# Local attention writes its result twice, and the linear attention takes its turned tokens from the second copy by GpSimd and VectorE

## The reference, cut to what matters

```
x = x + local_attention(group_norm(x))
t = tokens(x)                                   # 16 x 3136 x 128
t = t + linear_attention(ln(t), W, b)           # q,k = elu(.)+1; running sums of k v^T and k over t
t = t + recurrence(ln(t), W, V, gamma, beta)    # y = sigmoid(BN(W ln(t)) + V y), step by step
```

## Time and profile before

| | us |
|---|---|
| median of 3 runs | 1787.8 (1784.03 to 1788.23) |
| the profiled execution | 1784.76 |
| its span, first to last instruction | 1782.8 |
| TensorE / VectorE / ScalarE / GpSimd busy | 1749.7 / 1509.8 / 1269.8 / 1073.7 |
| mean granted clock of TensorE | 0.996 of full speed |

### The profile page before, as it was taken

How to read it: one execution, slowest core, us unless ns; L and a number is a source line. 1 busy time by engine, 2 the same in 40 slices (tenths; PEclk the granted TensorE clock), 3 DMA queues, 4 the chain that set the end, 5 groups by cost and what they waited for, 6 DMA issues and landing times.

```text
span 1782.8 us, 58142 instructions
## 1 busy us (share of the span) xinstructions
PE 1749.7 (98%) x19648; PEld 1587.7 (89%) x19648; DVE 1509.8 (85%) x4546; ACT 1269.8 (71%) x3387; POOL 1073.7 (60%) x1202
## 2 busy tenths in 40 slices
PE   7999999999999999989999999999999999989997
PEld 6888888888888888879999999999999999989997
DVE  7889888888888888778888888888888888868787
ACT  5877778887887788856666666666666666657776
POOL 6887888888888888843333333333333333368874
PEclk9999999999999999999999999999999999999999
DMA  5333343433333332313334434343434443457774
GB/s 167 105 103 104 104 110 99 109 107 102 110 103 104 106 106 70 83 43 70 73 67 68 70 68 70 68 67 68 70 68 70 68 68 70 86 178 277 291 278 176
DMA packets 361816, 188.30 MB, mean 106 GB/s; under 512 B 221760, under 2 KB 348720, under 8 KB 356656
## 3 DMA queue, kind: packets, MB, share of 16 engines
q1 hardware_dynamic: 360368, 183.40, 41.0%
q10 hardware_dynamic: 1152, 1.13, 0.2%
HBM read 106.58 MB, written 77.87 MB: 103 GB/s over the span
## 4 chain that ended last, share of the span: by engine, by line
PE 52%; issue 28%; POOL 17%; DVE 1%; DMA 1%; POOLq 0%; ACT 0%; ACTq 0%; SPq 0%; DVEq 0%
POOL la_rstd L1025 12%; PE k_psum L349 7%; PE k_psum L299 6%; PE k_psum L292 6%; PE k_psum L1488 6%; PE k_psum L317 6%; PE k_psum L333 6%; PE k_psum L365 5%; PE k_psum L1478 5%; PE k_psum L283 5%; POOL la_spread L1019 3%; POOL la_tn L1030 2%; DMA wa_group<-in_group 0%; POOLq L42 0%; DMA t<-la_tn 0%
## 5 line engine op out<-in xcount | busy, mean ns | idle before, releaser
L1019 POOL TENSOR_SCALAR la_spread<-la_mv 128x4 f32<-128x4 f32 (+1 forms) x203 | 46.2, 228 | 476.1 <-DVE la_mv L1130 476.0
L618 POOL TENSOR_TENSOR wa_prob<-wa_prob,wa_peak 128x784 f32<-128x784 f32 x128 | 195.0, 1523 | 116.8 <-DVE wa_peak L484 116.8
L966 ACT ACTIVATE la_ve<-k_psum 128x256 f32<-128x256 f32 x196 | 75.6, 386 | 231.9 <-PE k_psum L847 231.9
L1025 POOL TENSOR_TENSOR la_rstd<-la_spread,k_exponent 128x4 f32<-128x4 f32 (+1 forms) x203 | 207.8, 1024 | 17.2 <-POOL la_spread L1019 0.4
L625 POOL TENSOR_TENSOR wa_prob<-wa_prob,wa_inv 128x784 f32<-128x784 f32 x128 | 195.2, 1525 | 11.3 <-DVE wa_inv L445 11.3
L835 PE MATMUL k_psum<-la_uT,la_wt 128*128 128x256 f32 x784 | 201.9, 380 | 0.0
L1085 DVE SCALAR_TENSOR_TENSOR la_fqk<-k_psum,la_raised 128x512 f32<-128x512 f32 x196 | 135.4, 691 | 72.8 <-ACT la_raised L958 72.6
L1562 ACT ACTIVATE sc_y<-k_psum,sc_cols 128x128 f32<-128x128 f32 x414 | 152.3, 368 | 51.9 <-PE k_psum L1488 8.8
L476 DVE TENSOR_TENSOR wa_prob<-k_psum,wa_bias 128x784 f32<-128x784 f32 x128 | 124.9, 976 | 66.2 <-PE k_psum L317 66.1
L1488 PE MATMUL k_psum<-sc_y,sc_vT 128*128 128x128 f32 x824 | 171.0, 289 | 0.0
L958 ACT ACTIVATE la_raised<-k_psum,la_minus_one 128x512 f32<-128x512 f32 x196 | 134.8, 688 | 43.9 <-PE k_psum L835 43.7
(11 more groups left out here) (137 smaller groups left out, 5205.3 us busy)
## 6 DMA issues: line engine op xcount, KB each, us to landing
la_xc<-x SPq DMA_DIRECT2D x196, 128.0 KB, 3.0
wa_xT<-in_x_cm SPq DMA_DIRECT2D x124, 196.0 KB, 3.3
sc_tb<-t SPq DMA_DIRECT2D x17, 1320.0 KB, 8.3
out<-sc_ob SPq DMA_DIRECT2D x17, 1280.0 KB, 5.4
wa_xw<-in_x_tok SPq DMA_DIRECT2D x64, 224.0 KB, 2.7
wa_xw<-in_x_tok SPq DMA_DIRECT2D x64, 168.0 KB, 2.3
x<-wa_y SPq DMA_DIRECT2D x64, 168.0 KB, 2.8
x<-wa_y SPq DMA_DIRECT2D x48, 224.0 KB, 2.9
```

Of the source, the lines that this page charges most:

```text
L618: nc.gpsimd.tensor_tensor(s, s, peak[:, k % S, :].unsqueeze(2).broadcast_to([128, PAIRS * HEADS, WIN]), ALU.subtract).then_inc(lowered, 1)
L1025: nc.gpsimd.tensor_tensor(rstd[:, n % S, used], spread[:, used], exponent[:, used], ALU.pow).then_inc(rooted, 1)
```

## The change

The window stage stores each finished tile of tokens a second time, cut in four quarters of 32 channels, in a new DRAM tensor `quarters`. The linear stage loads from it with partition (quarter, i) and four consecutive tokens of 32 channels in each row, so that one VectorE transpose in squares of 32 x 32 gives all of a unit's tokens with channels on partitions. The norm's factors, 1/root and 1 - mean/root, are made by GpSimd with tokens on partitions, stored in a DRAM tensor `norms` and loaded again in the layout of the quarters. GpSimd multiplies and adds them in place (`stretch`, `displace`). TensorE's `turn_tokens`, ScalarE's `turned_out` and VectorE's `normalise` go. Loads and statistics run further ahead (units n+10 and n+8 in place of n+4 and n+3), the linear part is joined to fifteen window steps in place of nine, and stores of `t2` are no longer cut (`table_rows`).

```diff
 window_attention:
-        STORES = {wr: len(place(wr)) for wr in range(NWR)}
+        STORES = {wr: sum(1 + tiles for _, tiles, _, _, _ in place(wr)) for wr in range(NWR)}
-        JOIN = NU - 3
+        JOIN = NU - 9
                         sp.dma_start(dst, y[p:q, k, t:t + tiles, :]).then_inc(stored[k], 16)
+                        for i in range(tiles):
+                            first = n // NWR * T + token + i * (q - p)
+                            sp.dma_start(quarters[:, first:first + q - p, :].rearrange("k t r -> t k r"),
+                                         y[p:q, k, t + i, :].rearrange("p (k r) -> p k r", r=SQ)).then_inc(stored[k], 16)
 linear_attention:
-        XS = 8
-        AHEAD = 7
+        XS = 8
+        XC = 14
+        XL = 7
+        RS = 2
+        TS = 3
+        QS = 5
+        NS = 3
+        AHEAD = 12
+        def table_rows(c):
+            first, block = c * P, SQ * STEPS
+            return bass.AP(t2.tensor, (first % block * NB + first // block) * SF, [[NB * SF, P], [block * NB * SF, QUADS], [1, SF]])
-        steps = range(-4, UNITS + 9)
+        steps = range(-10, UNITS + 9)
 sync:
-                    at_least(sp, attended, n - XS + 1)
-                    sp.dma_start(xc[:, n % XS], rows(x1, n)).then_inc(loaded[n % XS], 16)
+                    at_least(sp, attended, n - XC + 1)
+                    at_least(sp, measured, n - XL + 1)
+                    sp.dma_start(xc[:, n % XC], rows(x1, n)).then_inc(loaded[n % XL], 16)
+                def load_quarters(n):
+                    at_least(sp, u_out, n - QS + 1)
+                    for a in range(2):
+                        first = (2 * n + a) * P
+                        sp.dma_start(xq[:, n % QS, a].rearrange("p j r -> p (j r)"),
+                                     bass.AP(quarters.tensor, first * SQ, [[B * T * SQ, QUADS], [QUADS * SQ, SQ], [1, QUADS * SQ]])
+                                     ).then_inc(q_loaded[n % QS], 16)
+                def store_norms(n):
+                    sp.wait_ge(shifted, n + 1)
+                    sp.dma_start(norms[n * 2 * P:(n + 1) * 2 * P, :].rearrange("(a p) s -> p a s", p=P), norm[:, n % S]).then_inc(n_stored[n % 2], 16)
+                def load_norms(n):
+                    sp.wait_ge(n_stored[n % 2], (n // 2 + 1) * 16)
+                    at_least(sp, normed, n - NS + 1)
+                    for a in range(2):
+                        first = (2 * n + a) * P
+                        sp.dma_start(nq[:, n % NS, a].rearrange("p j s -> p (j s)"),
+                                     bass.AP(norms.tensor, first * 2, [[0, QUADS], [2 * QUADS, SQ], [1, 2 * QUADS]])
+                                     ).then_inc(n_loaded[n % NS], 16)
-                    for a, p, q, col, s in pieces(n):
-                        sp.dma_start(dst, tn[p:q, n % XS, a]).then_inc(stored[n % XS], 16)
+                    for a in range(2):
+                        sp.dma_start(table_rows(2 * n + a), tn[:, n % XS, a]).then_inc(stored[n % XS], 16)
-                    load(n + 4)
-                    store(n - 5)
+                    load(n + 10)
+                    load_norms(n + 5)
+                    load_quarters(n + 6)
+                    store(n - 5)
+                    store_norms(n + 7)
 tensor:
-                    turn_tokens(n + 1)
 scalar:
-                    turned_out(n + 1)
 gpsimd:
+                    if inside(n, UNITS):                       # in statistics, behind the power
+                        nc.gpsimd.tensor_copy(norm[:, n % S, :, 0], rstd[:, n % S, 0:2]).then_inc(copied, 1)
+                        nc.gpsimd.tensor_tensor(norm[:, n % S, :, 1], mv[:, n % S, 0, :, 0], rstd[:, n % S, 0:2], ALU.mult).then_inc(lowered, 1)
+                        pool.wait_ge(copied, n + 1)
+                        pool.wait_ge(lowered, n + 1)
+                        nc.gpsimd.tensor_scalar(norm[:, n % S, :, 1], norm[:, n % S, :, 1], -1.0, 1.0, ALU.mult, ALU.add).then_inc(shifted, 1)
+                def stretch(n):
+                    nc.gpsimd.tensor_tensor(tokens, tokens, factors(n, 0), ALU.mult).then_inc(stretched, 1)
+                def displace(n):
+                    pool.wait_ge(stretched, n + 1)
+                    nc.gpsimd.tensor_tensor(tokens, tokens, factors(n, 1), ALU.add).then_inc(normed, 1)
-                    statistics(n + 3)
-                    remember(n + 3 - AHEAD)
+                    stretch(n + 3)
+                    displace(n + 3)
+                    statistics(n + 8)
+                    remember(n + 8 - AHEAD)
 vector:
+                def turn_tokens(n):
+                    dve.wait_ge(normed, n + 1)
+                    at_least(dve, qk_ready, n - TS + 1)
+                    at_least(dve, v_ready, n - TS + 1)
+                    nc.vector.transpose(uT[:, n % TS, :].rearrange("p (a t j) -> p a j t", a=2, j=QUADS), xq[:, n % QS]).then_inc(u_out, 1)
-                    normalise(n + 2)
-                    aggregate(n + 3)
+                    turn_tokens(n + 2)
+                    aggregate(n + 8)
```

More of the change, by code:

```diff
@@ L69, in build @@
     x1 = nc.dram_tensor("x1", (B, T, C), F32, kind="Internal").ap()
+    quarters = nc.dram_tensor("quarters", (QUADS, B * T, SQ), F32, kind="Internal").ap()
+    norms = nc.dram_tensor("norms", (B * T, 2), F32, kind="Internal").ap()
     t2 = nc.dram_tensor("t2", (C, STEPS, NB, SF), F32, kind="Internal").ap()
@@ L653, in _, with linear_attention @@
                 pipeline(step, **run, following=linear["gpsimd"](pool), join=JOIN + 1, prepare=(23, 24))
-def linear_attention(nc, ctx, x1, t2, attn_wt, attn_b, masks_d, ident, ones, exponent, gram, bank,
+def linear_attention(nc, ctx, x1, quarters, norms, t2, attn_wt, attn_b, masks_d, ident, ones, exponent, gram, bank,
                      ffn, signals, ffn_data):
@@ L702, in linear_attention @@
         folded = sem("la_folded")
-        loaded = [sem(f"la_loaded{i}") for i in range(XS)]
+        loaded = [sem(f"la_loaded{i}") for i in range(XL)]
+        q_loaded = [sem(f"la_q_loaded{i}") for i in range(QS)]
+        n_stored = [sem(f"la_n_stored{i}") for i in range(2)]
+        n_loaded = [sem(f"la_n_loaded{i}") for i in range(NS)]
         stored = [sem(f"la_stored{i}") for i in range(XS)]
@@ L723, in quads @@
             return tile.rearrange("p (q r) -> p q r", q=QUADS)
-        def pieces(n):
-            found = []
-            for a in range(2):
-                first = (2 * n + a) * P
-                token = first
-                while token < first + P:
-                    upto = min(first + P, (token // STEPS + 1) * STEPS)
-                    found.append((a, token - first, upto - first, token // STEPS, token % STEPS))
-                    token = upto
-            return found
+        def table_rows(c):
+            first, block = c * P, SQ * STEPS
+            return bass.AP(t2.tensor, (first % block * NB + first // block) * SF, [[NB * SF, P], [block * NB * SF, QUADS], [1, SF]])
         def stores_through(k, units):
-            return 16 * sum(len(pieces(m)) for m in range(k, units, XS))
+            return 32 * len(range(k, units, XS))
         def quotient_bank(n):
@@ L935, in tensor @@
                     if n == UNITS + 2:
-                        pe.wait_ge(u_out, UNITS)
+                        pe.wait_ge(*released["u"])
                         ffn.sum_weights(pe, b_u)
@@ L1110, in measure @@
                     if inside(n, UNITS):
-                        dve.wait_ge(loaded[n % XS], (n // XS + 1) * 16)
+                        dve.wait_ge(loaded[n % XL], (n // XL + 1) * 16)
                     if inside(n - AHEAD, UNITS):
@@ L1116, in measure @@
                             for a in range(2):
-                                tokens = tn[:, m % XS, a, :, 0:SQ] if which else xc[:, m % XS, a, :]
+                                tokens = tn[:, m % XS, a, :, 0:SQ] if which else xc[:, m % XC, a, :]
                                 last = nc.vector.bn_stats(stats[:, n % S, which, a, :], tokens)
```

98 lines of the change are left out of this document (44 added, 54 removed).

## The result

| | us |
|---|---|
| before, median of the runs beside it | 1785.91 (1782.45 to 1788.23) |
| after, median of 4 runs | 2414.57 (2412.72 to 2416.04) |
| ratio after to before | 1.3525, 95% interval 1.3507 to 1.3542 |
| span of the profiled execution after | 2412.8 |

The change costs 629 us. The forecast was 33 us less than before.

The account below looks back on a forecast made before the run. TensorE's order was taken to bound the linear stage, 3.98 us a unit falling to 3.76. -43 + 8 - 3 - 1 + 6 gave -33 from 1784.8: 1752, as median 1754 or 1755; range 1742 to 1828.

Parts of the forecast that it names:

- the two transposes: Linear stage: TensorE sets the 3.98 us period; removing two transposes saves 0.22 us a unit, 43 us over 196 units.
- the +6 for resources that disturb one another: Linear stage: 0.03 us a unit added for four resources that run near 3.6 us and disturb one another.
- The pair: Linear stage, GpSimd: two new tensor_tensor of 128x256 at 0.62 us each, bringing its sum to 3.58, upper end 3.7.
- rival 2: Linear stage: GpSimd is the bound, at 3.9 us a unit about -10 us, 1775; chance 0.14 (1768 to 1800).
- rival 4: Linear stage: the transposes weren't on the path, period stays 3.98, 1792; chance 0.04, shared with stores felt in the windows.
- VectorE's transpose: Linear stage: one new transpose of 128x256 taken at 0.40 us, at worst 0.67; VectorE's sum 3.48, at worst 3.75.
- the +8 and -3 of the sum: Join and draining steps: more GpSimd statistics in six window steps, +8 us; TensorE's waits for turned tokens go, -3.
- The windows' extra stores: Window steps: 3 or 4 more SP issues hide, DMA share rises from 0.36 to about 0.7; costed at nothing.
- Nothing waits: Linear stage, SP's queue: loads and stores land in 3.0 us, the store of norms has 7.5 us.
- the DMA term: Linear stage: 2048 packets a unit at 19 ns over 16 engines take 2.4 us of 3.76, share 0.65, covered.
- Rival 1: Linear stage: quarters and norms load through four DMA engines only, 3.7 to 4.3 us a unit; chance 0.26 (1790 to 1860).
- rival 3: Linear stage: SP is the bound, eight issues at 0.48 plus waits, 3.9 to 4.0 us, 1775 to 1795; chance 0.06.

Follow-up runs that it names:

- e5: The changed kernel with quarters laid out for one load at one stride, norms neither stored nor loaded, factors constant at 1: 1746.55 us, ratio 0.98.
- e6: The changed kernel with its own loads of quarters (slowest dimension 4), norms neither stored nor loaded, factors constant: 1746.11 us.
- e16: e5 with VectorE's transpose writing its output without a stride, tokens in another order: 1746.92 us.
- e13: e10 with the two loads of the factors issued from ScalarE's queue in place of SP's: 1758.18 us, ratio 0.9882 to the kernel before.
- e2: The changed kernel with only the quarters laid out for one load at one stride (slowest dimension 128), saving one issue a unit: 1959.38 us.
- e7: e5 with the norms stored in pieces of 8 B but never loaded: 1835.64 us.
- e9: e7 with each token's 8 B written to 64 B of its own in DRAM: 1759.50 us.
- e3: The kernel before with two more unread loads of 64 KB a unit, slowest DRAM dimension 4: 1815.78 us.
- e10: e2 with 64 B a token in the norms, stored and loaded, in place of 8 B: 1850.69 us.
- e12: e2 with norms still stored, but the factors' loads taken from old rows of `x1`: 2094.93 us.
- e11: The changed kernel with 64 B a token in the norms in place of 8 B, stored and loaded: 1969.62 us, ratio 1.1057 to the kernel before.
- e4: The kernel before with two more unread loads of 64 KB a unit, slowest DRAM dimension 128: 1782.68 us.
- e8: e5 with two loads a unit of 32 B pieces from old rows of `x1` and no norms stored: 1751.78 us.

## Why the prediction was wrong

*What bounds the kernel, and the two transposes: right.* e5 has TensorE gapless at 3.77 a unit. Its first and last store of `t` lie at 801.4 and 1529.0, so the stage takes 727.6, 44 less than before, for the -43 of the sum; the +6 for resources that disturb one another wasn't needed. e5 makes no trip, so this bears out the forecast for the change without the norms' transfers, and not for the change.

*GpSimd: right.* The pair took 0.62 each and the three small ones 0.19 to 0.20. TensorE stays gapless in e5 and e6, so rival 2 is out, and so is rival 4. By an estimate scaled from the figure of the Trainium skill (GPSIMD Engine Reference, Elementwise side-by-side cycle accounting), 4497 ns for 2048 columns, the pair would be 0.77 each; these rows disagree, as those of before did.

*VectorE's transpose: mis-sized, without effect.* 0.40 was chosen near half of 669 ns; contiguous it takes 0.445 and with the change's output stride 0.65. The step's own bound of 0.67 held it. VectorE's sum becomes 3.73, just under TensorE's period, and e16 shows that nothing hung on it.

*The join: right in e5* (+5, for the +8 and -3 of the sum). In the changed kernel it is +34; e13 has its first store of `t` at 809.1, +13.

*The windows' extra stores: right up to the join.* The DMA share there went from 0.36 to 0.61, forecast 0.7, and from 100 to 700 us TensorE works 598.66 us, where it had 598.65. In the join, where these stores meet the new transfers on SP's queue, the three steps that a store had to land didn't cover it: VectorE waits for one in eight steps.

```profile
DVE wa_y L461 <- DMA quarters<-wa_y: 33.8, 8, 7.6
```

It is 20.6 us in e13 and doesn't occur in e5. "I cost this at nothing" fails there, by a small part of the 629 us.

*The step that failed first: "`load_norms` waits for the store of norms issued two steps (7.5 us) before; a load lands in 3.0 us, a store I take to be alike. Nothing waits", with the DMA term behind it, where all 2048 packets of a unit got the mean price of 19 ns.* In the changed kernel that store lands in 7.1 us and the load of `x1` in 6.6, where both were taken at 3.0. The rows behind it were of loads of 512 B and stores of 132 B, the text took them for 8 B as well and drew no upper end from the distance. By the estimate above a stored piece of 8 B takes 93 ns of a DMA engine and not 19, so that the term, with the rest at 19, is (1792 x 19 + 256 x 93)/16 = 3.6 us of 3.76, where 2.4 stood. The wait that the sentence names is the smaller part of it. SP's waits for the store of norms, in the changed kernel and in e2:

```profile
SPq L815 <- DMA norms<-la_norm: 0.5, 1, 0.5
...
SPq L822 <- DMA norms<-la_norm: 33.3, 47, 2.5
```

In the changed kernel two steps have grown to 14 us; it is in e2, at 4.8 us a unit, that the landing reaches into SP's queue. The pieces of 8 B cost 89 us over e5 when they are stored side by side and nobody reads them, and 13 when each has 64 B of its own. Taking the whole trip away turns the changed kernel into one of 1746.11: 668 us are this step together with what it meets, the three issues of the trip included. The range couldn't hold this, since every case in it priced packets at the mean or below ("packets of 32 B should be cheaper than the mean").
The Trainium skill (DMA: Bandwidth & Descriptors, Specifications) puts full rate at 512 B or more and says that below it a read-modify-write is done. The runs bear out that small stores are dear; they don't bear out 512 B as the line that matters here, for 64 B at a time, still below it, takes 445 us off.
How the pieces lie decides most of their cost between e7 and e9, which store the same pieces for 89 and 13 us. That a store waits for another one to the same 64 B is a reading that fits; it is argued, not shown, and e9 also spreads a unit's factors over 16 KB in place of 2, which no run tells apart from it.

*Rival 1 was real, and not the cause by itself.* e3 costs 34 us, and the rival's stage at 4.15 was +33, but the two agree by luck. By the rival's own sum each of the four engines carries 80 + 64 = 144 packets in e3, 2.7 us at 19 ns, which is covered; and the kernel for which the +33 was made pays nothing for its quarters on four engines, as e6 shows. In the changed kernel a price appears only beside a trip: 76, 119, 290 or 455 us. This holds the engines together with the saved issue, which no run separates.

*SP was underpriced, a second step that failed.* The sum took eight issues at 0.43, 3.4 us, bounds 3.0 and 3.8. Loads with a DRAM side of three dimensions take 0.47 to 0.53 each, the uncut stores 0.50 in e10 (0.43 in e5); seven issues came to 3.87 in e10, eight would be near 4.4. By this estimate the change would have been some 80 us slower than before even without stretched issues (0.4 us above 3.98, 196 times), and rival 3 (0.06, 1775 to 1795) deserved far more and a higher price. Two issues fewer on SP are the last 93 us between e10 and e13. "An SP that is late by a microsecond hurts nobody, unless it is late every unit": it is late every unit.

*How it becomes 595 us.* One queue issues all of a unit's transfers in order, and two of its issues stretch to 3.5 us where transfers land late (that the queue is then full is argued, the length is shown). The load of `x1` is issued late and lands late; VectorE waits for it in 181 units (719.7 us), and TensorE behind VectorE. Slow pieces, few engines and a long list of issues cost more together than one by one: added to e13 singly they cost 144, 76 and 93 us, 313 in sum, and all three 656. How the 668 us split between the three, the table leaves open by its nature; why e12 is slower than e2 stays open too.

*The clock* reads as a consequence, and this is argued. TensorE's granted clock, the mean over the full level (2.4 GHz) and the lower one (1.2), is 0.87 in the stage where TensorE works 394 of 600 us, 0.94 in e12 with 232 of 300, and 1.00 in e5 with 300 of 300, but also 1.00 in e11 with 242 of 300. In the changed kernel TensorE waits for VectorE and isn't among the larger parts of the chain shown with the result.

## What to carry to other kernels

A small side product that goes through DRAM has to be priced by the size and the neighbourhood of its pieces, not by its bytes or by the mean packet: 2 KB in pieces of 8 B side by side cost 89 us, where two more loads of 64 KB a unit cost 1 us (e4), and giving each piece 64 B of its own took 76 of them away. Count the issues of the queue in the step's period, at the price of their own shape, before looking at the share of the DMA engines; and when one queue issues everything in order, test suspects together as well as singly, since a suspect that costs nothing alone (quarters loaded with 4 as the slowest dimension, in two issues: 1746.11 against 1746.55) was worth 455 us in company. The version to keep is e13, 1.2% faster than before; the trip through DRAM still costs 12 us of the 34 that e5 gains.

## What the runs showed of the hardware that was not expected

- 256 stored pieces of 8 B a unit, side by side, took the landing of 128 KB loads from 3.3 to 7.6 us and the kernel from 1746.55 to 1835.64; the same pieces 64 B apart left 1759.50, although landings stayed at 6.5 us and the DMA share at 0.88. In DMA engine time a stored piece comes to 93 ns side by side and 78 apart, a loaded one of 32 B to 16 (estimates from the queue's share in e5, e7, e9 and e8).
- Loads of the same bytes and rows cost 34 us with 4 as the slowest DRAM dimension and 1 with 128 (e3, e4); an issue of the first takes 0.54 us and of the second 0.46.
- An issue on SP takes 0.36 to 0.42 us for a plain load and 0.47 to 0.53 for one whose DRAM side has three dimensions (medians of e5, e6 and e10); a single store of `t` took up to 4.4 in the changed kernel.
- VectorE's transpose of 128x256 takes 445 ns written contiguously and about 650 with an output step of four elements.
